# A gated recurrence on one core: the last chunk's input projection in four parts of two steps

## What is computed

```
xz = x @ W_z ; xr = x @ W_r ; xh = x @ W          # for all steps: the projection
def step(h, (xzt, xrt, xht)):
    z  = sigmoid(xzt + h @ U_z + vz)              # v*: the condition's terms
    r  = sigmoid(xrt + h @ U_r + vr)
    hh = tanh(xht + (r * h) @ U + vh)
    h  = (1 - z) * h + z * hh
x = x + the sequence of h
```

## Time and profile before

| | us |
|---|---|
| median of 3 runs | 1593.16 (1592.95 to 1593.18) |
| the profiled execution's own time | 1593.21 |
| span from its first to its last instruction | 1591.3 |
| TensorE busy (share of the span) | 1573.7 (99%) |
| VectorE busy | 1383.0 (87%) |
| ScalarE busy | 829.5 (52%) |
| GpSimd busy | 214.0 (13%) |

### The profile page before, as it was taken

How to read it: one execution, slowest core, us unless ns; L and a number is a source line. 1 busy time by engine, 2 the same in 40 slices (tenths; PEclk the granted TensorE clock), 3 DMA queues, 4 the chain that set the end, 5 groups by cost and what they waited for, 6 DMA issues and landing times.

```text
span 1591.3 us, 47108 instructions
## 1 busy us (share of the span) xinstructions
PE 1573.7 (99%) x19742; PEld 1216.3 (76%) x19742; DVE 1383.0 (87%) x3188; ACT 829.5 (52%) x1868; POOL 214.0 (13%) x269
## 2 busy tenths in 40 slices
PE   9999999999999999999999999999999999999996
PEld 6888888888888767777777777777777777777886
DVE  5898999999888988888898888888988888888776
ACT  5999999999888743333333333333333333333322
POOL 0000000000000002222211112222222222211221
PEclk9999999999999999999999999999999999999999
DMA  6131324212241320110100101101011011000000
GB/s 215 54 106 54 106 80 133 80 54 79 77 136 51 129 88 2 55 56 2 55 28 29 55 2 55 56 2 56 17 40 55 2 55 55 2 29 2 30 29 29
DMA packets 46628, 89.15 MB, mean 56 GB/s; under 512 B 1744, under 2 KB 38096, under 8 KB 38864
## 3 DMA queue, kind: packets, MB, share of 16 engines
q1 hardware_dynamic: 46416, 86.13, 15.8%
HBM read 49.43 MB, written 36.70 MB: 54 GB/s over the span
## 4 chain that ended last, share of the span: by engine, by line
PE 97%; DVE 1%; ACT 0%; DMA 0%; issue 0%; SPq 0%; DVEq 0%
PE ps L905 33%; PE ps L960 29%; PE ps L988 17%; PE ps L976 16%; PE ps L923 2%; PE ps L878 1%; DMA raw<-in_x 0%; DVE ST L783 0%; PE ps L936 0%; DVE RL L817 0%; DVE ST L834 0%; DVE ST L818 0%; ACT ST L524 0%; ACT ST L522 0%; DVE HL L841 0%
## 5 line engine op out<-in xcount | busy, mean ns | idle before, releaser
L905 PE MATMUL ps<-XS,W 128*128 128x512 f32 x2304 | 526.5, 391 | 2.7 <-ACT XS L375 2.7
L905 PEld LDWEIGHTS ps<-XS,W 128*128 128x128 f32 x2304 | 434.1, 189 | 93.9 <-issue 2.6
L960 PE MATMUL ps<-XB,W 128*128 128x512 f16 (+1 forms) x1296 | 272.2, 356 | 0.0
L976 PEld LDWEIGHTS ps<-HL,U 128*128 128x128 f16 x6352 | 209.5, 98 | 34.7 <-issue 8.1
L960 PE MATMUL ps<-AR,W 128*128 128x512 f16 x1008 | 235.8, 379 | 0.0
L976 PE MATMUL ps<-HL,U 128*128 128x64 f16 x6352 | 224.1, 193 | 5.8 <-DVE HL L841 5.2
L988 PE MATMUL ps<-HL,U 128*128 128x64 f16 x4064 | 204.9, 204 | 0.0
L960 PEld LDWEIGHTS ps<-XB,W 128*128 128x128 f16 x1296 | 120.0, 97 | 97.0
L524 ACT ACTIVATE ST<-ST 128x256 f32<-128x256 f32 x127 | 52.9, 417 | 263.7 <-DVE ST L788 237.9
L522 ACT ACTIVATE ST<-ST 128x128 f32<-128x128 f32 x254 | 72.2, 309 | 217.9 <-DVE ST L783 217.7
L988 PEld LDWEIGHTS ps<-HL,U 128*128 128x128 f16 x4064 | 176.4, 98 | 0.0
(11 more groups left out here) (94 smaller groups left out, 1962.0 us busy)
## 6 DMA issues: line engine op xcount, KB each, us to landing
x_scratch<-AR SPq DMA_DIRECT2D x16, 1024.0 KB, 7.4
raw<-x_scratch SPq DMA_DIRECT2D x11, 1024.0 KB, 4.8
out_y<-raw SPq DMA_DIRECT2D x11, 1024.0 KB, 3.9
raw<-in_x SPq DMA_DIRECT2D x10, 1024.0 KB, 5.7
ST<-in_x SPq DMA_DIRECT2D x5, 1024.0 KB, 5.8
out_y<-AR SPq DMA_DIRECT2D x4, 1024.0 KB, 5.3
w_scratch<-U SPq DMA_DIRECT2D x3, 1024.0 KB, 4.8
W<-w_scratch SPq DMA_DIRECT2D x3, 1024.0 KB, 7.8
```

Of the source, the lines that this page charges most:

```text
L905: op = pe.matmul(ps[b][:, :], W[:, g, wp, k, e * P:(e + 1) * P], XS[:, c % 2, xp, k, :], start=n == 0, stop=n == 11)
L960: op = pe.matmul(ps[PB[i % 3]][:, 0:m], second_weights(W2_ORDER.index(g), wp, k, e), x, start=n == 0, stop=n == 11)
L976: pe.matmul(ps[b][:, col:col + B], U[:, g, uh, k, e * P:(e + 1) * P], S[:, k, 0], start=opens, stop=False, skip_group_check=True)
```

## The change

The last chunk is done in four parts (`PARTS = TC // 2`) of two steps. A matmul of a part has 128 columns (2 steps x 64 batches), read as 64 pieces of two elements. There are 4 x 144 = 576 of them where there were 288 of 256 columns. They are spread evenly over the fourteen steps 112 to 125, 41 or 42 a step. In these steps the first place takes 28 of them (`LAST_LOOK`), the second the other 13 or 14. One gate's four feature groups of a part now share one bank (4 x 128 columns), so that there are 12 banks to evacuate. Each is evacuated by two instructions, one for each of its two steps, of 4 x 64 elements per partition. Where the bank is complete within the first 28 fills, the first of these stands ahead of Z's add (`evacuate_first`) and the second at the end of the step (`evacuate_second`); otherwise both stand at the end. `number`, `xp_after` and `xp_ready` count the banks and evacuations anew.

```diff
+LAST_LOOK = 28
+PARTS = TC // 2
...
         def fills_of_step(t):
             j, tt = divmod(t, TC)
-            todo = fills(NCH - 1, 0) if j == NCH - 2 else fills(NCH - 1, 1) if j == NCH - 1 else fills(j + 1)
-            per = 2 * FILL if j == NCH - 1 else FILL
-            return todo[per * tt:per * (tt + 1)]
+            if j < NCH - 2:
+                return fills(j + 1)[FILL * tt:FILL * (tt + 1)]
+
+            todo = [item for part in range(PARTS) for item in fills(NCH - 1, part)]
+            i, n = t - TC * (NCH - 2), 2 * TC - 2
+            return todo[len(todo) * i // n:len(todo) * (i + 1) // n]
+
+        def look(t):
+
+            return LOOK if t < TC * (NCH - 2) else LAST_LOOK
...
-            def evacuate(j, part, g, e):
+            def evacuate(j, part, g, e, step=None):
...
+                if part is None:
+                    out = XP[j % 2][:, g, e].rearrange("p (t n) -> p t n", t=TC)
+                    src, v = by_step(ps[PB[i % 3]][:, :], B), V[:, g, e].unsqueeze(1).to_broadcast([P, TC, B])
+                else:
+                    out = XP[j % 2][:, g, :, (2 * part + step) * B:(2 * part + step + 1) * B]
+                    src, v = ps[PB[i % 3]][:, :].rearrange("p (e n t) -> p t e n", e=KT, t=2)[:, step], V[:, g]
...
+            def evacuate_first(t):
+                for j, part, g, e, k, wp, xp, n in fills_of_step(t)[:look(t)]:
+                    if n == 11 and part is None:
+                        evacuate(j, part, g, e)
+                    elif n == 11 and e == KT - 1:
+                        evacuate(j, part, g, e, 0)
...
-                for jj, part, g, e, k, wp, xp, n in fill[:LOOK]:
-                    if n == 11:
-                        evacuate(jj, part, g, e)
+                evacuate_first(t)
                 dve.wait_ge(s_Z, u + 1)
                 add_x(t, zg, Z, 0, (0, 1, 2, 3), s_zh, s_pz, u + 1)
...
-                    x = x.rearrange("p (n t) -> p n t", t=TC)[:, :, steps_of(part)]
-                m = 512 if part is None else 256
-                op = pe.matmul(ps[PB[i % 3]][:, 0:m], second_weights(W2_ORDER.index(g), wp, k, e), x, start=n == 0, stop=n == 11)
-                if n == 11:
+                    x, o = x.rearrange("p (n t) -> p n t", t=TC)[:, :, 2 * part:2 * part + 2], o[:, e * 2 * B:(e + 1) * 2 * B]
+                op = pe.matmul(o, second_weights(W2_ORDER.index(g), wp, k, e), x, start=n == 0, stop=n == 11)
+                if n == 11 and (part is None or e == KT - 1):
                     op.then_inc(s_prj, 1)
...
-                for item in fill[:LOOK]:
+                for item in fill[:look(t)]:
                     project(*item)
                 if u:
                     pe.wait_ge(s_pc, 2 * u)
                 recurrent_first(t, C, 2, RL, s_rhi)
                 pe.wait_ge(s_rlo, u + 1)
                 recurrent_second(t, C, 2, RL, s_C)
-                for item in fill[LOOK:]:
+                for item in fill[look(t):]:
                     project(*item)
```

More of the change, by code:

```diff
@@ L214, in fills_of_step, with xp_after @@
             j, tt = divmod(t, TC)
-            todo = fills(NCH - 1, 0) if j == NCH - 2 else fills(NCH - 1, 1) if j == NCH - 1 else fills(j + 1)
-            per = 2 * FILL if j == NCH - 1 else FILL
-            return todo[per * tt:per * (tt + 1)]
-        def number(j, part, g, e):
-            return 12 * (j - 1 + (part or 0)) + KT * W2_ORDER.index(g) + e
+            if j < NCH - 2:
[5 more added lines that the diff above has]
+            return LOOK if t < TC * (NCH - 2) else LAST_LOOK
+        def number(j, part, g, e):
+            if part is None:
+                return 12 * (j - 1) + KT * W2_ORDER.index(g) + e
+            return 12 * (NCH - 2) + 3 * part + W2_ORDER.index(g)
+        def xp_after(i):
+            return i + 1 + max(0, i + 1 - 12 * (NCH - 2))
         def xp_ready(t, g):
             j, tt = divmod(t, TC)
-            return number(j, 2 * tt // TC if j == NCH - 1 else None, g, KT - 1) + 1
+            return xp_after(number(j, tt // 2 if j == NCH - 1 else None, g, KT - 1))
         def is_joint(t, g):
             return t < JOINT and g != RESET
-        def steps_of(part):
-            return slice(0, TC) if part is None else slice(part * TC // 2, (part + 1) * TC // 2)
         CE = EARLY * BC
@@ L753, in _ @@
                 evacuate_b(n)
-            def evacuate(j, part, g, e):
+            def evacuate(j, part, g, e, step=None):
                 i = number(j, part, g, e)
-                tt = steps_of(part)
-                n = tt.stop - tt.start
                 if i == 0:
@@ L765, in evacuate, with evacuate_second @@
                 gi = W2_ORDER.index(g)
-                dve.scalar_tensor_tensor(out=XP[j % 2][:, g, e].rearrange("p (t n) -> p t n", t=TC)[:, tt],
-                                         in0=by_step(ps[PB[i % 3]][:, 0:n * B], B), scalar=dx1[:, 3 + gi:4 + gi],
-                                         in1=V[:, g, e].unsqueeze(1).to_broadcast([P, n, B]),
-                                         op0=ALU.mult, op1=ALU.add).then_inc(s_xp, 1)
+                if part is None:
+                    out = XP[j % 2][:, g, e].rearrange("p (t n) -> p t n", t=TC)
[3 more added lines that the diff above has]
+                    src, v = ps[PB[i % 3]][:, :].rearrange("p (e n t) -> p t e n", e=KT, t=2)[:, step], V[:, g]
+                dve.scalar_tensor_tensor(out=out, in0=src, scalar=dx1[:, 3 + gi:4 + gi], in1=v,
+                                         op0=ALU.mult, op1=ALU.add).then_inc(s_xp, 1)
+            def evacuate_first(t):
[4 more added lines that the diff above has]
+                        evacuate(j, part, g, e, 0)
+            def evacuate_second(t):
+                for j, part, g, e, k, wp, xp, n in fills_of_step(t)[:look(t)]:
+                    if n == 11 and part is not None and e == KT - 1:
+                        evacuate(j, part, g, e, 1)
+                for j, part, g, e, k, wp, xp, n in fills_of_step(t)[look(t):]:
+                    if n == 11 and part is None:
+                        evacuate(j, part, g, e)
+                    elif n == 11 and e == KT - 1:
+                        evacuate(j, part, g, e, 0)
+                        evacuate(j, part, g, e, 1)
             def add_x(t, dst, b, g, es, s_high, s_done, count):
@@ L794, in _ @@
                 Hp, Hn = Hst[(t + 1) % 2], Hst[t % 2]
-                fill = fills_of_step(t)
                 u = t - 1
@@ L807, in _ @@
                     dve.tensor_tensor(hlo, Hn, hhi, ALU.subtract).then_inc(s_hlo, 1)
-                    for jj, part, g, e, k, wp, xp, n in fill:
-                        if n == 11:
-                            evacuate(jj, part, g, e)
+                    evacuate_first(t)
+                    evacuate_second(t)
                     continue
@@ L851, in _ @@
                     dve.tensor_tensor(hlo, Hn, hhi, ALU.subtract).then_inc(s_hlo, 1)
-                for jj, part, g, e, k, wp, xp, n in fill[LOOK:]:
-                    if n == 11:
-                        evacuate(jj, part, g, e)
+                evacuate_second(t)
                 if 3 <= tt < 7 and j + 2 < NCH:
@@ L942, in project @@
                 i = number(j, part, g, e)
-                if n == 0:
+                if n == 0 and (part is None or e == 0):
                     if i < 3:
@@ L946, in project @@
                     else:
-                        pe.wait_ge(s_xp, i - 2)
+                        pe.wait_ge(s_xp, xp_after(i - 3))
                     if g == W2_ORDER[0] and e == 0 and not part:
@@ L955, in project @@
                         pe.wait_ge(s_lastlo, 4)
-                x = XB[j % 2][:, xp, k]
+                x, o = XB[j % 2][:, xp, k], ps[PB[i % 3]][:, :]
                 if part is not None:
-                    x = x.rearrange("p (n t) -> p n t", t=TC)[:, :, steps_of(part)]
-                m = 512 if part is None else 256
-                op = pe.matmul(ps[PB[i % 3]][:, 0:m], second_weights(W2_ORDER.index(g), wp, k, e), x, start=n == 0, stop=n == 11)
-                if n == 11:
+                    x, o = x.rearrange("p (n t) -> p n t", t=TC)[:, :, 2 * part:2 * part + 2], o[:, e * 2 * B:(e + 1) * 2 * B]
+                op = pe.matmul(o, second_weights(W2_ORDER.index(g), wp, k, e), x, start=n == 0, stop=n == 11)
+                if n == 11 and (part is None or e == KT - 1):
                     op.then_inc(s_prj, 1)
```

## The result

The changed kernel takes 1615.9 us (median of 4 runs, 1615.62 to 1616.29), the kernel before in the same comparison 1593.06. The ratio is 1.0142, with a 95% interval of 1.013 to 1.0155. It is 22.8 us slower, where +2.1 was forecast and 1599.0 was the end of the range. It is the far end of the first rival, fills of 113 ns each (1616).

What follows compares the result with a forecast made beforehand. The step's dependent chain, with two TensorE holes, was taken to set the beat. Stall removed -7.2, fills in the first hole +9.2, evacuations +0.1 gave +2.1 us on 1593.16: 1595.3 us, range 1592.8 to 1599.0.

Steps and rivals of the forecast that it cites:

- the first rival: Fills before the first RL matmul cost over 62.5 ns: 17% up to 70 ns (1599.2 us), 6% at 113 ns (1616).
- What bounds the stage: Steps 113 to 124: full clock, beats of 6.80 us with 18 fills a step, 8.60 with 36.
- the two holes: TensorE's waits in step 114: before the first RL matmul (0.67 us), and from RL's end to the next step (1.83).
- the stall of 1.80: Steps 120 to 123: 36 fills overfill the second hole, 1.80 us a step; removing this gives -7.2 us.
- What does one cost? ... I take 56 + 4 = 60 ns: Price of a new 128-column fill in pieces of two: 60 ns, low end 56, high end 113.
- The Trainium skill's rule on lines: SBUF reads 16-byte lines; full rate needs at least two hits a line, and each new line pays a penalty.
- The Trainium skill's 81 ns at N = 128: Sustained weight load and matmul at 128 columns, about 81 ns each, would make the sum +10.4 us; trace showed 55.6.
- 28 x price - 1.02: Lengthening of each step 112 to 125 by 28 fills before RL: 0.66 us at 60 ns, +9.2 in all.
- +0.05 in steps 116 and 123: An evacuation delays Z's add, so GpSimd's product runs beside t1 again: +0.05 us each, together +0.1.
- The second hole: TensorE between the RL matmuls' end and the next step: 1.83 us, of which 13 or 14 fills take under 0.9.
- t1 freed from GpSimd's product: VectorE's t1, now later than GpSimd's product: its first half takes 0.28 us instead of 0.43.

Runs made afterwards that it cites:

- the idle matmuls: Kernel before with 24 wide fills a step over steps 112 to 123, plus idle 256-column matmuls in the last four steps: 1586.89 us, ratio 0.996.

## Why the prediction was wrong

- **What bounds the stage, the two holes, the stall of 1.80:** right. The beats of 8.60 are gone, and no kernel with an even spread of wide or cheap fills has them.
- **"What does one cost? ... I take 56 + 4 = 60 ns":** this step failed, and it alone. It measured 115. I read the 4 ns by which 256 columns in pieces stand above the line of the contiguous ones as a surcharge on the columns. They were the tip of another limit: 64 lines at 1.8 ns are 113 to 115, just above the 109 that 256 columns take in one piece (as the idle matmuls did). As the new fills touch the same 64 lines, they cost the same. One row could not tell a surcharge from a floor; it needed a second width over the same lines, and no such row was there. The text had 113 as an end of the cost and gave it 6%, outside the range. Two readings of one number deserved chances nearer to each other.
- **The Trainium skill's rule on lines** (SBUF — State Buffer, Specifications (TRN2)): read as the prediction read it, that two hits in a line are enough for full rate, it is contradicted by these runs. Two hits gave 115 ns, four gave 58, eight gave 56. That each line costs is borne out, though not as the small penalty on top that the prediction took from it.
- **The Trainium skill's 81 ns at N = 128** (TensorE: Matmul & The Clock Gate, Back-to-back issue gap) is contradicted by the contiguous fills, 56 ns with their loads.
- **28 x price - 1.02:** right. At 115.4 ns it gives 2.21, measured 9.04 - 6.80 = 2.24; at 56 ns 0.55, measured 7.36 - 6.80 = 0.56. So is +0.05 in steps 116 and 123: 1515.33 - 1506.24 = 9.09 in 116. Had the price been known, the sum would have been 14 x 2.21 - 7.1 = +23.8 (1617), against +22.8 in the medians and +24.1 between the HL rows.
- **The second hole:** 13 fills still fit at 115 ns (13 x 0.115 = 1.50 of the 1.59 us from 1496.04 to 1497.63); 14 of them, in step 118, just don't, and the next beat is 9.08. That a swallowed delay shortens it I had not seen; it didn't matter for the forecast, only for two of the experiments' expectations.
- **t1 freed from GpSimd's product:** borne out. The two halves take 0.55 together where they took 0.63 (the earlier trace rows has the first at 0.43).

## What to carry to other kernels

Before a matmul's operand is cut narrower, count the 16-byte lines that it touches, and not its columns: in a layout that interleaves the steps, half the steps in a part means twice the matmuls at the same price each. Where work is moved into the idle places of a dependent chain, add the places up as one budget with what the chain swallows, and check the spread against it; here 24 wide fills a step fit to within 0.12 us, and gave 0.3 to 0.4% with no new layout. And a number that lies a little off a line may be a second limit just showing: price the change once with it as a surcharge, and once as a floor.

## What the runs showed of the hardware

- TensorE read its moving fp16 operand at 1.8 ns per 16-byte line (226 ns for 128 lines, 115 to 118 for 64, 58 for 32), whatever the number of pieces; with fewer lines the columns bind (56 ns for 128, with 16 lines).
- Four VectorE instructions that each write (and read, as one operand) 128 fp16 elements per partition with 128 bytes between them took 2.62 us, beside four such writes of ScalarE, where one instruction of 512 contiguous ones took 0.83.
- In a tail with TensorE busy 9.27 of 12.68 us the granted clock fell to 0.50 in one profile; it cost 1.5 us (a step of 8.34 in place of 6.81). In the kernel before, with TensorE busy 9.27 of 13.79 us in steps 125 and 126, it did not fall, so what made it fall stays open.
